# State scan of a decoder block: states and tokens summed by TensorE, the sum copied by ScalarE, the softplus correction in one VectorE operation

## What is computed

```
delta = softplus((xn @ W_delta) @ W_dt + b_dt)      # xn: layer norm of x, [16, 256, 256]
Bm, Cm = xn @ W_B, xn @ W_C                         # 16 states
dA  = exp(delta[..., None] * A)
dBx = delta[..., None] * Bm[:, :, None, :] * xn[..., None]
h = dA_t * h + dBx_t                                # over the 256 tokens of a batch
y = sum over the states n of h[n] * C_t[n]
x = x + y + D * xn
```

## Time and profile before

| | us |
|---|---|
| three runs | 1358.32, 1355.41, 1356.62; median 1356.62 |
| profiled execution | 1355.57, of which the span is 1353.8 |
| state scan in the span | from 0 to about 520 |
| busy in the span: TensorE, VectorE, GpSimd, ScalarE | 1038.2, 904.0, 648.5, 574.4 |
| VectorE's scans (L522), 256 | 297.9 |
| GpSimd's products (L413), 127 | 296.3 |

### The profile page before, as it was taken

The page is one execution under the profiler, slowest core; times in us unless marked ns, Lnnn a source line. Parts: engine busy times, 40 slices in busy tenths (PEclk is TensorE's granted clock), DMA queues, the critical chain, the costliest instruction groups (busy, mean ns, idle before and its releaser), DMA issues. The chain is left out here.

```text
span 1353.8 us, 20753 instructions
## 1 busy us (share of the span) xinstructions
PE 1038.2 (77%) x6769; PEld 921.5 (68%) x6769; DVE 904.0 (67%) x2041; ACT 574.4 (42%) x1282; POOL 648.5 (48%) x591
## 2 busy tenths in 40 slices
PE   4767878788777875776557674699999999999970
PEld 3656868677676764666215563599999988888860
DVE  6999999999999994888887564233323232322328
ACT  4768787777878653443504342122112121111110
POOL 4887888878697742000102555343444434343420
PEclk8999999999999997555878796799999999999985
DMA  8544556565655522123030110787887888888829
GB/s 250 187 136 135 181 150 183 151 190 161 177 169 157 177 68 65 31 36 59 34 124 32 32 40 25 238 281 263 276 277 263 269 263 283 257 271 269 273 93 350
DMA packets 163531, 232.62 MB, mean 172 GB/s; under 512 B 34380, under 2 KB 87996, under 8 KB 162656
## 3 DMA queue, kind: packets, MB, share of 16 engines
q1 hardware_dynamic: 145808, 207.79, 48.9%
q0 software_dynamic: 11280, 19.06, 4.2%
q10 hardware_dynamic: 6336, 4.44, 1.0%
HBM read 203.08 MB, written 23.95 MB: 168 GB/s over the span
## 5 line engine op out<-in xcount | busy, mean ns | idle before, releaser
L1011 PE MATMUL st_y_ps<-ident,st_hc 128*128 128x128 f32 x2048 | 274.0, 292 | 113.3 <-DVE st_hc L530 113.3
L1011 PEld LDWEIGHTS st_y_ps<-ident,st_hc 128*128 128x128 f32 x2048 | 255.6, 203 | 135.9 <-DVE st_hc L530 134.9
L413 POOL TENSOR_TENSOR st_u<-st_dx,codes 128x1024 f32<-128x1024 f32 x127 | 296.3, 2359 | 40.6 <-DVE st_h L522 31.6
L522 DVE TENSOR_TENSOR_SCAN st_h<-st_da,st_u 128x512 f32<-128x512 f32 x256 | 297.9, 1205 | 0.2 <-POOL st_u L413 0.2
L2216 PE MATMUL mo_h<-mo_xt,w 128*128 128x128 f32 (+17 forms) x2048 | 281.4, 289 | 1.9 <-DVE mo_xt L2318 1.9
L2216 PEld LDWEIGHTS mo_h<-mo_xt,w 128*128 128x128 f32 x2048 | 271.0, 193 | 6.3 <-issue 2.5
L2324 DVE TENSOR_TENSOR mo_inter<-mo_silu,mo_h 128x128 f32<-128x128 f32 (+17 forms) x256 | 75.7, 304 | 281.0 <-ACT mo_silu L2290 219.3
L2156 POOL DMA_INDIRECT outs<-mo_o,choice x95 | 93.4, 983 | 232.0 <-DVE mo_o L2335 218.4
L2290 ACT ACTIVATE mo_silu<-mo_h 128x128 f32<-128x128 f32 (+17 forms) x256 | 71.5, 290 | 312.2 <-PE mo_h L2216 206.6
L749 ACT ACTIVATE st_da<-st_delta,st_a_neg 128x510 f32<-128x510 f32 x256 | 171.9, 685 | 57.6 <-DVE st_h L522 53.2
L530 DVE TENSOR_TENSOR st_hc<-st_h,st_cps 128x1024 f32<-128x1024 f32 x128 | 152.8, 1194 | 0.0
(11 more groups left out here) (359 smaller groups left out, 1414.0 us busy)
## 6 DMA issues: line engine op xcount, KB each, us to landing
codes<-bc SPq DMA_DIRECT2D x256, 256.0 KB, 3.7
w<-in_L_ffn_w_dram SPq DMA_DIRECT2D x128, 512.0 KB
wo<-in_L_ffn_wo_dram SPq DMA_DIRECT2D x64, 512.0 KB
co_got<-outs SPq DMA_DIRECT2D x16, 512.0 KB, 6.1
wave<-dist SPq DMA_DIRECT2D x16, 274.0 KB
x<-in_x_dram SPq DMA_DIRECT2D x8, 512.0 KB, 9.2
st_cx<-in_ctx_dram SPq DMA_DIRECT2D x8, 512.0 KB, 4.1
dist<-st_dd SPq DMA_DIRECT2D x32, 128.0 KB, 3.4
```

Source lines behind the costliest of these rows:

```text
L413: nc.gpsimd.tensor_tensor(u_sb[k % URING][:, :, :], dx[p % 2][:, :, :], over_chunks(b_sb[k % BRING]), ALU.mult).then_inc(u_ok, 1)
L522: nc.vector.tensor_tensor_scan(h_sb[k % HRING][:, dh, :], da_ps[dh][:, :], u_sb[k % URING][:, dh, :], 0.0, ALU.mult, ALU.add).then_inc(h_o ...
L1011: m = nc.tensor.matmul(y_ps[t // 2][:, t % 2, dh * P:(dh + 1) * P], hc_sb[k % RING][:, dh, t * P:(t + 1) * P], K.ident[:, :], start=False, ...
```

## The change

- `add_y` goes. TensorE opens the accumulators with four products of the tokens of x with the identity (128 x 256 each) beside the diagonal's, so that x is in the sum, and ScalarE copies the two banks over x (`take_y`), in slot 0 behind `decay` and `take_c`.
- `whole` of pairs 1 to 7 goes to ScalarE (`whole_z`, in slot 11 ahead of `take_st`) and leaves 1 + e; `lost` of these pairs moves on VectorE from slot 10 to slot 12 and does minus one and minus e in one operation; `soft` subtracts.
- The loads of x for pairs 1 to 7 share one semaphore, and every `mean` from `mean(1)` on waits for all seven.
- In the expert part GpSimd's constants count on a semaphore of their own.

```
-        x_in = [sem(f"x_in{g}") for g in range(NP)]
+        x_in = [sem("x_in_first"), sem("x_in_rest")]
...
-                dve.wait_ge(x_in[p], 16)
+                dve.wait_ge(x_in[min(p, 1)], 16 * (NP - 1) if p else 16)
...
-                nc.gpsimd.tensor_tensor(delta[p % 2][:, :, :], lz, az, ALU.add).then_inc(soft_ok, 1)
+                nc.gpsimd.tensor_tensor(delta[p % 2][:, :, :], lz, az, ALU.subtract).then_inc(soft_ok, 1)
...
-                nc.vector.tensor_scalar(az, ez, 1.0, -1.0, ALU.add, ALU.add).then_inc(whole_ok, 1)
+                nc.vector.tensor_scalar(az, ez, 1.0, None, ALU.add).then_inc(whole_ok, 1)
...
-                nc.vector.scalar_tensor_tensor(out=az, in0=az, scalar=-1.0, in1=ez, op0=ALU.mult,
-                                               op1=ALU.add).then_inc(lost_ok, 1)
+                nc.vector.scalar_tensor_tensor(out=az, in0=az, scalar=-1.0, in1=ez, op0=ALU.add,
+                                               op1=ALU.subtract).then_inc(lost_ok, 1)
...
-            def add_y(p, h):
-                dve.wait_ge(summed, (p + 1) * N)
-                rows = K.x[:, p * PTT + h * 2:p * PTT + h * 2 + 2, :]
-                nc.vector.tensor_tensor(rows, rows, y_ps[h][:, :, :], ALU.add).then_inc(x_ok, 1)
...
-                if n == 0 and real(p - 1):
-                    add_y(p - 1, 0)
-                    add_y(p - 1, 1)
...
-                if n == 10 and real(p + 1):
-                    whole(p + 1)
+                if n == 12 and real(p + 1):
                     lost(p + 1)
...
+            def whole_z(p):
+                nc.scalar.activation(az, ez, ACT.Copy, bias=1.0).then_inc(whole_ok, 1)
...
+            def take_y(p, h):
+                act.wait_ge(summed, (p + 1) * N)
+                nc.scalar.activation(K.x[:, p * PTT + h * 2:p * PTT + h * 2 + 2, :], y_ps[h][:, :, :], ACT.Copy
+                                     ).then_inc(x_ok, 1)
...
+                if n == 0 and d:
+                    take_y(p - 1, 0)
+                    take_y(p - 1, 1)
...
                 if n == 11:
+                    if a and p + 1 > 0:
+                        whole_z(p + 1)
...
+                        nc.tensor.matmul(y_ps[t // 2][:, t % 2, :], K.ident[:, :], tile(p, t), start=(t % 2 == 0),
+                                         stop=False)
```

More of the change, by code:

```diff
@@ L288, in load_x @@
                 sp.dma_start(K.x[:, p * PTT:(p + 1) * PTT, :],
-                             K.x_dram[p * PT:(p + 1) * PT, :].rearrange("(t p) d -> p t d", p=P)).then_inc(x_in[p], 16)
+                             K.x_dram[p * PT:(p + 1) * PT, :].rearrange("(t p) d -> p t d", p=P)).then_inc(x_in[min(p, 1)], 16)
             def load_ctx(p):
@@ L588, in open_delta @@
                 dve.wait_ge(lost_ok, 1)
-                nc.vector.tensor_tensor(delta[0][:, :, :], lz, az, ALU.add).then_inc(soft_ok, 1)
+                nc.vector.tensor_tensor(delta[0][:, :, :], lz, az, ALU.subtract).then_inc(soft_ok, 1)
                 dve.wait_ge(soft_ok, 1)
@@ L624, in _ @@
                     mean(p + 2)
-                if n == 10 and real(p + 1):
-                    whole(p + 1)
+                if n == 12 and real(p + 1):
                     lost(p + 1)
             p, u = LASTP, LASTP % 2
-            add_y(p, 0)
-            add_y(p, 1)
             mean_d(p)
@@ L889, in _ @@
             p = LASTP
+            take_y(p, 0)
+            take_y(p, 1)
             rough_scale_d(p)
@@ L1003, in total @@
                     for t in range(PTT):
+                        nc.tensor.matmul(y_ps[t // 2][:, t % 2, :], K.ident[:, :], tile(p, t), start=(t % 2 == 0),
+                                         stop=False)
                         for dh in range(DC):
                             nc.tensor.matmul(y_ps[t // 2][:, t % 2, dh * P:(dh + 1) * P],
-                                             xt[p % 2][:, dh, t * P:(t + 1) * P], diag[:, dh, :],
-                                             start=(t % 2 == 0 and dh == 0), stop=False)
+                                             xt[p % 2][:, dh, t * P:(t + 1) * P], diag[:, dh, :], start=False,
+                                             stop=False)
                 pe.wait_ge(hc_ok, k + 1)
@@ L1610, in expand @@
         late_of_ps, late_at_ps = bank(rank_ps[1])[:, 0:LATE], bank(rank_ps[1])[:, 2 * P:2 * P + LATE]
-        constant = sem("ex_constant")
+        constant, pool_raw = sem("ex_constant"), sem("ex_pool_raw")
         reach_ok, apart_ok, mask = sem("ex_reach_ok"), sem("ex_apart_ok"), sem("ex_mask")
@@ L1623, in expand @@
         tile = lambda t: K.x[:, t, :]
-        ALL = 12 + len(ROOMS) + 1
+        ALL = 12
         real = lambda b: 0 <= b < B
@@ L1654, in routing_constants @@
                                    [[-step, n // run_], [0, run_]], base=first, channel_multiplier=0,
-                                   **imprecise).then_inc(constant, 1)
-                nc.gpsimd.memset(before[:, :], 1.0).then_inc(constant, 1)
-                pool.wait_ge(constant, len(ROOMS) + 1)
+                                   **imprecise).then_inc(pool_raw, 1)
+                nc.gpsimd.memset(before[:, :], 1.0).then_inc(pool_raw, 1)
+                pool.wait_ge(pool_raw, len(ROOMS) + 1)
                 nc.gpsimd.affine_select(out=before[:, :], in_=before[:, :], compare_op=ALU.is_gt, fill=0.0,
```

## The result

| | before | after |
|---|---|---|
| median of four runs, us | 1357.18 | 1409.40 |
| profiled span, us | 1353.8 | 1405.0 |
| first scan begins | 27.22 | 29.36 |
| last pair's last product on VectorE (L530) begins | 498.89 | 547.54 |
| statistics of the last pair (L541 / L536) begin | 505.34 | 557.43 |

The change makes the kernel slower by 3.8% (ratio 1.0384, interval 1.0364 to 1.0403), 52.2 us by the medians. The predicted 1398 us was 11 us short; the direction and the place were right. The table says where it lies: 2.1 us before the first scan, 46.5 in the eight pairs, 3.4 between the last product and the statistics that follow. Some 1.5 us of these come back before the next part (the alignment), which begins 50.6 us later, at 579.81 instead of 529.21; that is nearly the whole of the 51.2 us of the span.

A forecast was written before the change was run, and what follows sets the result against it. VectorE was taken to bound the scan, with 0.28 us to spare from `lost` to the next pair's scan. 40.0 - 8.4 + 7.7 + 2.4 = +41.7 us gave 1398 us by the median, range 1384 to 1410.

The forecast's parts named there:

- The bound: In the scan, VectorE sets the pace, and the end of `lost` releases GpSimd's `soft` and sets the next pair's beginning.
- The chain, +40.0 us: GpSimd's work from `soft` to u of step 16: `lost` two slots later delays that scan 5.9 us a pair, +40.0 us.
- `add_y` and `whole` off VectorE: At pair ends, dropping `add_y` keeps -8.4 us over seven pairs; `whole`'s 5.0 us is swallowed by the wait for u.
- `take_y`, +7.7 us: ScalarE's copies in slot 0 wait for TensorE's sum of step 15, delaying step 18's decay: 1.1 us a pair, +7.7 us.
- Rival C: TensorE's half clock costs each pair 2.3 us at `take_y` and up to 1 behind it: 1407 to 1414 us, chance 0.10.
- The opening, +2.4 us: Before the first scan, `mean(1)` waits for the shared semaphore's last load at 17.6 us, delaying `take_z`: +2.4 us.
- The end, 0: Behind the last pair, ScalarE's two copies take as long as the removed `add_y` with its wait for TensorE: 0 us.
- The four products more per pair: On TensorE behind `products`' second half, 2.06 us a pair, hidden: 0, though half clock could show up to 1 us.
- A: At pair ends, `soft` need not wait for `lost`, so VectorE keeps its relief: -6.1 us, 1350.5 us, chance 0.05.
- B: GpSimd runs faster while VectorE stands, returning some 3.2 us a pair, 22 in all: 1376 us, chance 0.07.

The follow-up runs named there:

- `lost` alone: The kernel before with only `whole` moved to ScalarE and `lost` to slot 12, with the change's arithmetic; 1409.2 us, ratio 1.0387.
- the last version: Changed kernel with pair 1's load on its own semaphore, last `take_y` before `take_d`, `whole` (ScalarE) and `lost` in slot 10, other `take_y` in slot 1; 1347.96 us.
- `lost` back: The changed kernel with `whole` and `lost` on VectorE in slot 10 again, all else of the change kept; 1358.85 us, ratio 1.0016.
- both ends mended: The changed kernel with pair 1's load on its own semaphore and, behind the last pair, `take_y` ahead of the `take_d` waiting for `products`; 1403.87 us.

## Why the prediction was right, and where it was short

*The range.* The measured 1409.40 lies 0.6 us under the upper end of the range and above the forecast's own ends, 1392 to 1407. What took it in was the 8 us allowed for an error in the chain, and the chain had no such error. The direction, the bound and the chain were foreseen; that the range held is in part luck.

*The bound.* That VectorE sets the pace and that `lost` releases `soft` held. `soft` begins 0.13 us behind `lost` in both kernels, though the page names "issue"; the kernels with `lost` in slots 10 and 11 settle it, with 0.12 and 0.13.

*The chain, +40.0 us.* It held to a few hundredths. I had put the scan of step 16 at T + 21.2; with T at 269.17 + 1.11 = 270.28 (the product of step 10 begins at 269.17, and 1.11 later the next instruction would start) it begins at 291.54, T + 21.26. The two waits were to be 1.5 and 5 us and are 1.46 and 4.82. `lost` alone made +53.5 us, of which VectorE's wait for L413 is 42.9. One reading was a little off: 2.32 us is the distance from one u to the next, and a single u lasts 2.358, so the room before the scan was about 0.24 us and not 0.28.

*`add_y` and `whole` off VectorE.* The 8.4 us are kept, but swallowed by new waits; `whole` on ScalarE takes 1.04 us and delays nothing that shows. In the last version most of both savings arrives in the time: it is 9.7 us faster than before, of 13.4.

*`take_y`, +7.7 us: this is the step that failed.* "I take 1.1 us between 0.7 and 1.6" was too little: the profile has 13.1 us of waiting for the decay, 1.9 a pair, between 1.2 and 2.6. TensorE at half clock after standing for `add_squares` was right as a mechanism, but I let it act on the sum of step 15 and on `take_y` alone. It is `products` that ran at half clock, 4.6 to 6.0 us in six pairs instead of 3.1; the prediction had these rows, and priced half clock at the 1.6 us of one sum. ScalarE's `take_d` in slot 15 waits for `products`, and stands ahead of the decay of step 17, so that scan waits too (2.15 us in the pair shown), for which the sum had nothing. Of the 13.1 us, 8.3 stand there, before the scan of step 17, and 4.8 where I had put 7.7, before that of step 18. The two are not independent: with `take_d` out of the way the wait comes back behind `take_y`. Without the clock's part the price is the 0.6 us a pair of the kernel with `lost` back, against my 0.7. Rival C, with a chance of 0.10, had the size of it, but at `take_y` and behind it.

*Waits cost a little more than they show.* Without a wait, one VectorE instruction begins about 0.09 us before the one ahead of it ends; behind a wait it does not. The waits for u and decay are 28 in the page's count, so some 2.5 us (an estimate from these rows) come on top of 43.1 + 13.1 - 8.4 - 5.0 = 42.8. In each of the seven pairs the scan of step 12 also begins late, by a wait too short for a bracket: 270.51 instead of 270.28 in the pair shown, some 1.6 us in all. That makes 46.9, against the measured 46.5 us.

*The opening, +2.4 us.* 2.1 by the trace. `mean(1)` begins at 17.61 with the landing of the last load, where I had put 17.6.

*The end, 0: this term was missed.* "I count nothing" overlooked ScalarE's order: `take_d` in slot 15 of the last pair waits for `products`, which TensorE there does behind all the sums, and `take_y` stands behind it. First before, then the changed kernel:

```profile
504.02 1.28 DVE L536 TENSOR_TENSOR x<-x,st_y_ps 128x512 f32<-128x512 f32 x2 [2.80 <-PE st_y_ps L1011]
```

```profile
555.68 0.47 ACT L818 ACTIVATE st_dd<-st_w,st_aa 128x256 f32<-128x256 f32 x1 [8.79 <-PE st_w L997]
557.43 1.40 DVE L536 BATCH_NORM_STATS2 st_stats_d<-x 128x6 f32<-128x256 f32 x4 [7.58 <-ACT x L765]
```

VectorE's statistics wait 7.58 us, 3.4 more in all than `add_y` and its wait had taken. The kernel with both ends mended gives the opening and this back, 5.5 us together.

*The four products more per pair* cost nothing that a run shows while `take_y` stands in slot 0: in the kernel with `lost` back VectorE has no other wait in the pairs than that for the decay. With `take_y` a slot later they stand in the opening of the accumulators ahead of the 1.75 us wait; how much of it is theirs was not measured.

*The rivals.* A fell with the kernel with `lost` alone. B fell in the trace: while VectorE stood, L401 took 2.35 us, and of all the u of the changed kernel none took less than 2.339 (2.340 before):

```profile
L413 POOL TENSOR_TENSOR st_u<-st_dx,codes x127: 2339/2357/2384, 29.5 to 534.3; 128x1024 f32<-128x1024 f32 x127
```

The Trainium skill's "SBUF — State Buffer", section "SBUF: two separate sides", says of the ports that VectorE and GpSimd share that VectorE takes them only in a two-port mode or with two inputs in SBUF. These rows agree: scans and products with an input in PSUM did not hold GpSimd up, and their pause gave it nothing.

The Trainium skill's "TensorE: Matmul & The Clock Gate", section "HAM oscillation — how this bites in real kernels", says that a burst behind a long enough idle gap starts at the low clock. The changed kernel's `products` agree, with a granted clock of 0.50 behind 3.99 us. In the pair shown the sum of step 15, to which the prediction put the rule, ran at full clock again (1.00 from 296 us on).

## What to carry to other kernels

An instruction that is moved on the busy engine must be asked who waits for its end, and how much room the chain behind it has: here about a quarter of a microsecond, so two slots later was a loss of 40 us, and the relief of the busy engine was no relief. A wait of one engine spreads: TensorE stood, lost its clock, and ScalarE's in-order list carried that to the scan, a quarter of the waiting in all, and about half of that quarter was the clock's. An engine's list is also to be read at its two ends, where an instruction that is harmless in the middle may stand behind one that waits.

## What was not expected of the hardware

The length of the half clock, and that it differs from pair to pair. In the pair shown, after TensorE had stood for 3.99 us, the granted clock was 0.50 from about 289 us into `products` until about 295, so that nearly all of `products` ran at half speed (6.0 us instead of 3.1). I had counted on 0.9 us of it showing. This pair is the longest of six: behind stands of 4.1 to 5.5 us the others took 4.6 to 5.5, so the longer stand did not make the longer half clock. Behind the same 2.2 us, with `lost` in slot 11, five pairs ran at full clock and one did not. What decides it, no run here shows.
